# A two-layer graph kernel on one core: one spill slot instead of two, eight bit planes instead of fourteen, and gathers of the second layer moved ahead

## What is computed

```python
h = jnp.maximum(_layernorm(x, axis=-1), 0.0)
x = x + _L0_gnn_ref(h, adj, L0_gnn_weight, L0_gnn_att_weight)   # attention, 4 heads, softmax over neighbours
h = jnp.maximum(_layernorm(x, axis=-1), 0.0)
x = x + _L1_gnn_ref(h, adj, ...)   # agg = adj @ h; msg = relu(agg @ W_msg.T + b); a GRU cell on (msg, h)
```

## Time and profile before

| | |
|---|---|
| median of 3 runs | 1417.33 us (1415.73 to 1418.2) |
| the profiled execution, own time | 1415.82 us |
| its span, first to last instruction | 1414.0 us |
| mean granted PE clock | 0.732 |
| busy: PE, DVE, ACT, POOL | 811.3, 685.2, 657.6, 534.3 us |
| mean DMA rate over the span | 216 GB/s |

### The profile page before, as it was taken

How to read it: one execution, slowest core, us unless ns; L and a number is a source line. 1 busy time by engine, 2 the same in 40 slices (tenths; PEclk the granted TensorE clock), 3 DMA queues, 4 the chain that set the end, 5 groups by cost and what they waited for, 6 DMA issues and landing times.

```text
span 1414.0 us, 14221 instructions
## 1 busy us (share of the span) xinstructions
PE 811.3 (57%) x4397; PEld 614.5 (43%) x4397; DVE 685.2 (48%) x2956; ACT 657.6 (47%) x662; POOL 534.3 (38%) x549
## 2 busy tenths in 40 slices
PE   2667263837474664738374554738264552274997
PEld 1556152725353553636253443527154430142564
DVE  6667072727355362817264462727174500143675
ACT  2777272737464563738374563727223200022442
POOL 2112706152341506052332506061607577576400
PEclk9988666768676766758686766767666575576999
DMA  9999766849595957758595957667101122122201
GB/s 331 420 419 422 301 245 253 330 170 366 199 364 207 356 227 275 293 206 357 182 383 187 382 205 299 267 232 297 33 3 31 31 53 52 39 61 58 55 30 38
DMA packets 56749, 306.10 MB, mean 216 GB/s; under 512 B 14561, under 2 KB 32179, under 8 KB 40288
## 3 DMA queue, kind: packets, MB, share of 16 engines
q1 hardware_dynamic: 27936, 274.74, 48.5%
q0 software_dynamic: 18144, 23.62, 6.8%
q10 hardware_dynamic: 10592, 6.82, 1.6%
HBM read 296.70 MB, written 12.71 MB: 219 GB/s over the span
## 4 chain that ended last, share of the span: by engine, by line
another core or an unknown queue 29%; PE 29%; DVE 23%; issue 10%; DMA 4%; ACT 3%; POOL 1%; ACTq 0%; POOLq 0%; DVEq 0%
PE ps L860 6%; PE ps L953 3%; PE ps L951 3%; DVE after_off L1455 2%; DMA x<-in_x 2%; PE ps L1056 2%; DVE cand L1287 2%; PE ps L1054 2%; PE ps L893 2%; ACT ind L605 1%; DVE xb L1406 1%; PE ps L1065 1%; PE ps L1074 1%; PE ps L1075 1%
## 5 line engine op out<-in xcount | busy, mean ns | idle before, releaser
L605 ACT ACTIVATE ind<-adj_in 128x4144 bf16<-128x4144 int32 (+1 forms) x128 | 461.9, 3609 | 24.4 <-DMA adj_in<-in_adj 14.8
L516 POOL DMA_INDIRECT val<-in_adj,val_idx x160 | 162.1, 1013 | 519.7 <-DVE val_idx L1476 475.2
L860 PE MATMUL ps<-ind,bit_w 128*128 128x296 bf16 (+1 forms) x1792 | 311.0, 333 | 42.9 <-issue 21.9
L860 PEld LDWEIGHTS ps<-ind,bit_w 128*128 128x128 bf16 x1792 | 199.9, 113 | 133.9 <-ACT ind L605 27.3
L507 POOL DMA_INDIRECT rows_in<-wh_table,idx x192 | 193.4, 1007 | 105.4 <-issue 105.4
L558 POOL DMA_INDIRECT adj_in<-g_table,idx x145 | 141.8, 978 | 67.6 <-issue 43.0
L1436 DVE COPY off<-ps 128x8 f32<-128x8 f32 x16 | 2.6, 165 | 334.1 <-remote 334.0
L893 PE MATMUL ps<-pm,own 128*128 128x8 f32 x128 | 29.1, 356 | 203.7 <-DVE pm L1375 203.7
L630 ACT COPY pm<-pm 128x32 f32<-128x32 f32 x16 | 3.5, 217 | 274.5 <-DVE pm L1375 274.5
L893 PEld LDWEIGHTS ps<-pm,own 128*128 128x128 f32 x128 | 27.7, 319 | 209.4 <-DVE pm L1375 209.4
L1602 DVE SCALAR_TENSOR_TENSOR after_off<-ps,bias_in,after_off 128x512 f32<-128x512 f32 x16 | 12.0, 750 | 157.3 <-remote 57.7
(11 more groups left out here) (261 smaller groups left out, 1642.7 us busy)
## 6 DMA issues: line engine op xcount, KB each, us to landing
adj_in<-in_adj SPq DMA_DIRECT2D x64, 2072.0 KB
adj_in<-in_adj SPq DMA_DIRECT2D x64, 2024.0 KB
wh_table<-rows_in POOLq DMA_DIRECT2D x16, 264.0 KB, 8.7
g_table<-t_buf ACTq DMA_DIRECT2D x16, 256.0 KB
out<-rows_in SPq DMA_DIRECT2D x16, 256.0 KB
rows_in<-wh_table,idx POOLq DMA_INDIRECT x192
val<-in_adj,val_idx POOLq DMA_INDIRECT x160
adj_in<-g_table,idx POOLq DMA_INDIRECT x160
```

The source lines that it names most:

```text
L516: nc.gpsimd.indirect_dma_start(out=val2[:, s, k:k + 1], out_offset=None, in_=adj_values, in_offset=bass.IndirectOffsetOnAxis(ap=val_idx2[: ...
L605: nc.scalar.activation(ind[:, t % 2, a:b], adj_in[:, slot, 0:b - a].bitcast(I32), ACT.Relu, bias=1.0, scale=-1.0, accum_out=empty[:, bass. ...
L860: ins = nc.tensor.matmul(o[:, 0:w], bit_w[:, b, :], ind[:, t % 2, c0:c0 + w], start=False, stop=(b == BITS - 1))
```

## The change

- Bit planes: 8 instead of 14, 1024 words a tile; each half holds whole planes. PE packs with 2 x (1 + 8) matmuls of 512 columns a tile instead of 2 x (1 + 14) of 296. A segment of `search` has 256 words instead of 148.
- Patterns lie in a ring of three half tiles; ACT waits for the piece three before. The fourth quarter of `ind` (`edges_scan`) takes gathered rows.
- The two halves share one spill slot of 128 edges: `E2` is 9, a unit of the later half has 4 gathers, of the earlier one 5. Bases of the earlier half start where the later half's end.
- `scan_rows`: the later half's units of groups 0 to 3 are fetched during the scan, one group behind `rows(s)` for s = 10 to 13. In the drain the later half's units of groups 4 to 7 are fetched (before: of groups 0 to 2). The last stage issues 112 gathers instead of 145.

```diff
-BITS = 14
+BITS = 8
-WORDS = 592
+WORDS = N // BITS
...
-E2 = 10
+E2 = 9
+SLOTS_OF = (5, 4)
-PRE = 3
+PRE = 4
+SCAN_PRE = 4
+EARLY = SCAN_PRE + PRE
+IND = 3
+FIRST_SCAN = NG // 2 + 2
...
         def unit(q, h):
-            return q if h and q < PRE else (PRE + q if q < PRE else 2 * q + 1 - h)
+            return PRE + q if not h and q < EARLY else q - SCAN_PRE if q < EARLY else 2 * q - SCAN_PRE + 1 - h
 
         def group_of(n):
-            return n if n < PRE else (n - PRE if n < 2 * PRE else n // 2)
+            return SCAN_PRE + n if n < PRE else n - PRE if n < PRE + EARLY else (n + SCAN_PRE) // 2
...
+                def scan_rows(q):
+                    for k in range(SLOTS_OF[1]):
+                        nc.gpsimd.indirect_dma_start(
+                            out=edges_scan[:, q, k, :], out_offset=None, in_=g_table[0:HN, :],
+                            in_offset=bass.IndirectOffsetOnAxis(ap=idx2[:, q, 5 + k:6 + k], axis=0),
+                        ).then_inc(scan_landed[q], 16)
...
                     rows(s)
-                for par in range(2):
-                    pool.wait_ge(g_out[par], 16 * (NG // 4))
+                    if s == FIRST_SCAN:
+                        for par in range(2):
+                            pool.wait_ge(g_out[par], 16 * (NG // 4))
+                    if 0 <= s - FIRST_SCAN < SCAN_PRE:
+                        scan_rows(s - FIRST_SCAN)
...
-                    if not isinstance(tile, int) or tile >= 2:
-                        act.wait_ge(pack_done, tile - 1)
+                    if tile * 2 + half >= IND:
+                        act.wait_ge(pack_done, tile * 2 + half - IND + 1)
...
                     for n in range(G):
-                        link(V.tensor_tensor(base2[:, :, n + 1], base2[:, :, n], spill[:, :, n], ALU.add))
-                    V.tensor_scalar(valid2[:, :, G], base2[:, :, G], pid_low[:, 0:1], None, ALU.is_gt)
-                    V.tensor_reduce(checks[:, 4, s:s + 1], base2[:, :, G], AX.X, ALU.max)
+                        V.tensor_tensor(base2[:, 0, n + 1:n + 2], base2[:, 0, n:n + 1], spill[:, 0, n:n + 1], ALU.add)
+                        link(V.tensor_tensor(base_early[:, n + 1:n + 2], base_early[:, n:n + 1], spill[:, 1, n:n + 1], ALU.add))
+                    V.tensor_scalar(late_place[:], base2[:, 0, G:G + 1], pid_low[:, 0:1], None, ALU.is_gt)
+                    link(V.tensor_scalar(base2[:, 1, :], base_early[:], base2[:, 0, G:G + 1], None, ALU.add))
+                    V.tensor_scalar(valid2[:, 0, G:G + 1], base2[:, 1, G:G + 1], pid_low[:, 0:1], None, ALU.is_gt)
+                    V.tensor_copy(checks[:, 4, s:s + 1], base2[:, 1, G:G + 1])
...
-                            nc.tensor.matmul(o, r[:, G, :], w[:, G:2 * G, :].rearrange("p k r -> p (k r)"), start=(h == 1), stop=False)
                             for t in range(G):
...
+                            if h == 0:
+                                ins = nc.tensor.matmul(o, r[:, G, :], w[:, G:2 * G, :].rearrange("p k r -> p (k r)"), start=False, stop=True)
```

More of the change, by code:

```diff
@@ L143, in gat_gru_kernel @@
         base2 = sb("base2", [P, 2, G + 1])
+        base_early = sb("base_early", [P, G + 1])
+        late_place = sb("late_place", [P, 1])
+        place_diff = sb("place_diff", [P, 1])
         off2 = sb("off2", [P, 2, 2, G])
@@ L399, in gat_gru_kernel @@
         edges_landed = [sem(f"edges_landed{i}") for i in range(RING2)]
+        scan_landed = [sem(f"scan_landed{i}") for i in range(SCAN_PRE)]
         agg2_mm = sem("agg2_mm")
@@ L424, in unit, with landed @@
         def unit(q, h):
-            return q if h and q < PRE else (PRE + q if q < PRE else 2 * q + 1 - h)
+            return PRE + q if not h and q < EARLY else q - SCAN_PRE if q < EARLY else 2 * q - SCAN_PRE + 1 - h
         def group_of(n):
-            return n if n < PRE else (n - PRE if n < 2 * PRE else n // 2)
+            return SCAN_PRE + n if n < PRE else n - PRE if n < PRE + EARLY else (n + SCAN_PRE) // 2
+        def landed(n):
+            return sum(16 * SLOTS_OF[1 if m < PRE or m >= PRE + EARLY and (m - SCAN_PRE) % 2 == 0 else 0] for m in range(n % RING2, n + 1, RING2))
         def turn_bank(q):
@@ L556, in message_rows_of @@
                             pool.wait_ge(agg2_mm, group_of(n - RING2) + 1)
-                        for k in range(5):
+                        for k in range(SLOTS_OF[h]):
                             nc.gpsimd.indirect_dma_start(
@@ L570, in _ @@
                 with pool.Else():
+                    for q in range(SCAN_PRE):
+                        pool.wait_ge(scan_landed[q], 16 * SLOTS_OF[1])
                     for n in range(PRE):
-                        pool.wait_ge(edges_landed[n], 16 * 5)
+                        pool.wait_ge(edges_landed[n], landed(n))
                     for par in range(2):
@@ L937, in neighbours2 @@
                     nc.tensor.matmul(ps_shift(s), shift[:], send2[:].rearrange("p g c -> p (g c)"), start=True, stop=True)
-                    nc.tensor.matmul(ps_wrap(s), wrap[:], send2[:, 0:G - 1, :].rearrange("p g c -> p (g c)"), start=True, stop=True) \
+                    nc.tensor.matmul(ps_wrap(s), wrap[:], send2[:].rearrange("p g c -> p (g c)"), start=True, stop=True) \
                         .then_inc(shift_mm, 1)
@@ L951, in send_lists2 @@
                             nc.tensor.matmul(ps_list2(s)[:, h * 5 + t, :], after_off[:, h, t, :], dsend[:, t, :], start=True, stop=True)
-                        for t in range(G):
-                            ins = nc.tensor.matmul(ps_list2(s)[:, h * 5 + G, :], after_off[:, h, G + t, :],
-                                                   dsend_over[:, t - 1, :] if t else dsend[:, 0, :], start=(t == 0), stop=(t == G - 1))
+                    for n in range(2 * G):
+                        ins = nc.tensor.matmul(ps_list2(s)[:, G, :], after_off[:, n // G, G + n % G, :],
+                                               dsend_over[:, n % G, :] if n else dsend[:, 0, :], start=(n == 0), stop=(n == 2 * G - 1))
                     ins.then_inc(list2_mm, 1)
```

79 lines of the change are left out of this document (41 added, 38 removed).

## The result

The changed kernel takes **1423.84 us** (median of 20 runs, 1412.61 to 1429.75), the kernel before beside it 1415.58 us (20 runs, 1410.21 to 1423.25): ratio 1.0045, 95% interval [1.0028, 1.0063], slower by some 6 us by the ratio and by 8 us by the medians. Predicted were 1410 us and faster. The profiled execution took 1419.17 us, its span is 1417.4 us, the mean clock 0.725.

A forecast was written before the change was run, and what follows sets the result against it. The prediction took the scan to be bound by POOL's gather bursts followed by DVE's chain. Its terms, +1.4 + 28 - 2.5 - 34 = -7.1 us, gave a median of 1410 us, range 1384 to 1434.

The forecast's parts named there:

- What bounds the kernel: Scan: a loop of POOL's gather burst, DVE's release behind it, then DVE's chain; in the last stage without gathers, PE.
- Gathers in the scan: Scan bursts: one gather fewer in nine steps, three more in four, two fewer in the last, at 1.40 us: +1.4 us.
- DVE's chain: Scan steps: wider searches and more linked small instructions on DVE cost 2.0 us a step, 28 us in 14 steps.
- Drain: After the scan: two gathers fewer in the second run, two more hidden in the last, 0.3 for DVE: -2.5 us.
- Start: Up to 120 us the loads bind, so the changed packing was to cost 0 us there.
- Last stage: From its first gather to the end: 287.7 us to become 254 us with fewer gathers and matmuls, -34 us.
- half pace: Last stage: PE's assumed speed on group sums beside POOL's first run of 62 gathers, putting group 4's sum at t0 + 110.
- The change does what it says: Rival feared otherwise: over-full spill slots send the kernel down another path; chance put at nothing.
- Ring waits: Rival, last stage: PE's signals come 4 us late at five ring waits, giving back 20 us: 1430 us; chance 0.22.
- PE held by number of instructions: Rival, scan: PE passes bursts at a fixed instruction pace, so fewer instructions save 9.2 us a step: 1282 us; chance 0.04.
- Gathers in the scan hidden: Rival, scan: the 16 gathers moved there cost nothing, -22 us: 1388 us; chance 0.16.

The follow-up runs named there:

- e4: Changed kernel with POOL waiting after every fifth gather of steps 1 to 14 until the gathers have landed: 1183.53 us, 0.838 of the kernel before.
- e17: Changed kernel with a short break (POOL clears a tile of its own) after every third gather of steps 1 to 14: 1146.31 us, 0.812 of the kernel before.
- e16: Changed kernel unaltered, rerun as yardstick in a job where the kernel before takes 1412.77 us: 1417.84 us, ratio 1.002.
- e3: Changed kernel with four more gathers of adjacency values, results unused, in every step: 1456.38 us, 1.026 of the kernel before.
- e18: Changed kernel without `scan_rows`, in a job where the kernel before takes 1412.77 us: 1402.09 us, 0.993 of the kernel before.
- e1: Changed kernel without `scan_rows`, in a job where the kernel before takes 1411.8 us: 1372.31 us, 0.974 of the kernel before.
- e2: Changed kernel without `scan_rows` and with the pattern's ring at four pieces again: 1378.98 us, 0.973 of the kernel before.
- e6: Kernel before with POOL waiting after every fifth gather of the scan until they land, where the unaltered one takes 1043.7 us: ratio 1.091.
- e14: Changed kernel unaltered, in a job where the kernel before takes 1043.4 us: 0.9953 of the kernel before.
- e13: Kernel before unaltered, run for its trace in a job where it takes 1043.4 us: ratio 0.9997.
- e9: Changed kernel unaltered, as yardstick in a job where the kernel before takes 1044.27 us: 0.9957 of the kernel before.
- e10: Changed kernel without `scan_rows`, in a job where the kernel before takes 1044.27 us: 1.011 of the kernel before.
- e12: Changed kernel with a short break after every third gather of steps 1 to 14, where the kernel before takes 1044.27 us: 0.994 of it.

## Why the prediction was wrong

**What bounds the kernel** was read right and not to its end. The loop of burst, release, chain is there, the tail of the earlier trace rows holds in the trace after to 0.4 us, and e4 and e17 show that breaks in the issuing end nearly all of the hold in the scan. The prediction took PE's packing for a part of that wait and did not ask when line 933 ran; it had run at 619.59, 8.8 us before DVE went on. I took the hold as given and looked for the change's effect inside it; the breaks are worth 270 us in a holding job, the whole change a few.

**Gathers in the scan, +1.4 us.** Taken with the chain's 2.0 us a step, the prediction gives 8 x (2.0 - 1.4) = +4.8 for the eight steps of the table, 4 x (4.2 + 2.0) = +24.8 for the four with 25 gathers, and -0.8 for the last. Measured +6.1, +22.6 and -2.5: right in the recorded trace. The price itself is no constant: 1.4 there, 1.0 in e16, about 0.5 in e3, since PE's signals sometimes come out before the burst's end.

**DVE's chain, 2.0 us a step.** Right. From DVE's release to the next first gather it was 32.8 and is now 35.3 in the step shown; the mean idle time between the bursts of the scan grew from 35.9 to 38.0. By parts: from `offsets2` to `differences2` 6.47 to 7.15 us (+0.7, predicted 0.6), `edges2` 2.34 to 2.62 (+0.3, predicted 0.3), the rest +1.1 (predicted 1.0 and 0.1), MAX8 416 ns (predicted 426).

**Drain, -2.5 us: this step failed.** It measured +8.9, where two gathers fewer were to give a gain. I costed the drain by POOL's gathers and never asked when PE's signals would come out there. Before, the signal for the last `differences2` slipped out in mid-burst; in the new order it came behind the burst's end, and POOL's last values waited 20.5 us instead of 8.2 for the lists that hang on it. The traces of e16 and e18 show the same, 14.6 and 14.5 us at that line, and so do e1, e2 and e3 (16.5, 15.1 and 20.8). The kernel before has one trace from a holding job, so it is not shown that the signal slips out there every time, nor that the order of the gathers is the reason: PE came to its line 16.7 us into the burst before and 20.5 us into it now, and no run separates the two.

**Start, 0 us: this term failed too, and its cause is open.** I put it at nothing because the loads bind there. The first burst came 6.7 us later. The kernel before has it at 131.7 and 130.5 in its two traces, but e6, whose start is the same program, at 139.9; the changed kernel's traces have it at 135.3 to 143.2, with eight planes alone it was 135.0. Some 4 us may come with the planes, which I had put down as hidden by the loads; the spread of the start is as large, so no cause is shown. The ring of three is not it (e2).

**Last stage, -34 us.** Right in size: -38.3, with the points on the way at t0 + 104.5 for the end of the long stop (110 predicted), + 130.6 for the last run (138), and 8.15 us a group (8.5). Why PE is slow beside the first run I had left as "half pace". The timeline shows it, two rows of many:

```profile
1203.79 0.37 PE L1082 MATMUL ps<-adj_in 128*128 128x128 f32 x1 [2.43 <-issue]
1206.59 0.37 PE L1082 MATMUL ps<-adj_in 128*128 128x128 f32 x1 [2.43 <-issue]
```

From 1195 to 1221 us PE starts one matmul every 2.8 us and waits for nothing that the profile shows; e14, a free job, has 1.4 us of such idle time at this line in all.

Sum: +6.7 + 28.6 - 2.5 + 8.9 - 38.3 = +3.4 us between the profiled executions, where -7.1 was forecast. Start and drain, put at 0 and -2.5, make 18 us of the difference; the scan (26.1 for 29.4) and the last stage (-38.3 for -34) give 8 of them back. By the medians the change is at +8 us, and of the further 5 us no trace tells. In the other holding job it is 1.002 [0.999, 1.005], so that its loss is clear of noise in one of two such jobs.

**The rivals.** The change does what it says: the last stage issues 112 gathers. Ring waits: ruled out, POOL's last run began before t0 + 138, not at 158. PE held by number of instructions: half right. In the trace before, PE is slowed in a burst, with 64.6 us of idle time before line 880 in which it waits for nothing shown (0.5 us or less in e13, a free job), and from the second burst on comes to line 933 only 17 to 26 us after a burst's first gather; in the trace after it comes to line 955 after 10 to 12 us, as in the free e13 and e14. So the change did free PE in the steps of the scan, and it gained nothing, since the signal comes out no sooner: DVE's wait per step did not shrink. Gathers in the scan hidden: wrong where PE is held, right in free jobs, where e9 against e10 gives the 16 gathers 16 us of worth. So the rule of the Trainium skill ("DMA: Bandwidth & Descriptors", rules for kernel authors) to issue early and wait late is borne out by those runs and not by the recorded one.

## What to carry to other kernels

When an engine waits for "remote" until just behind another engine's long row of issues, first test the row itself: a few lines that break it up told more, and gained more, than the whole rewrite. Then compare when the awaited instruction ran with when the waiting engine went on: a gap of 18.5 us here said that work was not what was missing. A gain forecast at half a per cent needs a row for every part of the program, the start and the drain too. And run the yardstick in every job: the same kernel was 1.002 of the one before in one job and 0.995 in another, by the record's number on the same chip 12.

## What had not been expected of the hardware

- The same program runs at 1412 to 1416 us in some jobs and at 1043 to 1044 in others. In the first sort PE's signals come out late behind POOL's indirect DMAs when these are issued 0.30 us apart; in the second DVE goes on 0.5 us after the start of PE's line (e13, e14). The record has chip 12 in both sorts (e9 to e12, e16 to e18), so the chip alone does not decide it. What does is open; nothing else about the jobs is on record.
- In a holding job a break of 1.1 us after three gathers (e17) is enough to let the signals out; breaks until landing, 3 to 6 us after five (e4), do it too and cost more. How many gathers in a row do no harm was not tried beyond three and five.
- It is not PE's signals alone. In the drain of the trace after, while POOL gathers, DVE waits for its own instruction in a linked add, which in the earlier trace rows takes 0.04 to 0.05 us:

```profile
1106.24 0.16 DVE L1466 TENSOR_TENSOR base<-base,spill 128x1 f32<-128x1 f32 x1 [0.94 <-DVE base_early L1467]
```

  And ACT's copy for the second table, which by the code waits for PE's line 944 (it ran at 1106.79), goes on within 0.1 us of DVE, 3.3 us behind the last gather:

```profile
1126.25 0.58 ACT L648 COPY t_buf<-ps 128x512 f32<-128x512 f32 x1 [24.47 <-remote]
```

- A wait's releaser is told as "remote" where PE's signal is held and by PE's line where it is not: the same wait reads 337.9 us in e16 and 51.4 us in e14.
